# Another order of the groups, evictions and transfers in the fused stage of a Mamba and mixture-of-experts layer

## The reference

```
h = layernorm(x) * (1 + ca) + sa
x = x + ga * mamba(h)
h = layernorm(x) * (1 + cb) + sb
x = x + gb * moe(h)
```

```
delta = softplus(dt @ dt_proj_w.T + dt_proj_b)
h_t = exp(delta_t * A) * h_(t-1) + delta_t * u_t * B_t
y_t = sum over the 16 states of h_t * C_t
out = (y * silu(res)) @ out_proj_w.T
```

## Time and profile before

| | |
|---|---|
| median of 3 runs | 2546.36 us |
| the profiled execution | 2546.36 us, its span 2544.5 us |
| TensorE, VectorE, GpSimd, ScalarE busy | 2219.1, 1938.2, 1934.6, 1400.8 us |
| mean granted TensorE clock | 0.896 |
| DMA, mean | 88 GB/s |

### The profile page before, as it was taken

The page is one execution under the profiler, slowest core; times in us unless marked ns, Lnnn a source line. Parts: engine busy times, 40 slices in busy tenths (PEclk is TensorE's granted clock), DMA queues, the critical chain, the costliest instruction groups (busy, mean ns, idle before and its releaser), DMA issues. The chain is left out here.

```text
span 2544.5 us, 31166 instructions
## 1 busy us (share of the span) xinstructions
PE 2219.1 (87%) x7664; PEld 1058.8 (42%) x7665; DVE 1938.2 (76%) x2068; ACT 1400.8 (55%) x2474; POOL 1934.6 (76%) x830
## 2 busy tenths in 40 slices
PE   7769898999989898989898999989866639999997
PEld 3223343434434343444343434434333435565664
DVE  2799899998989898989899999989898162222222
ACT  3666666667575767667566667675745222222221
POOL 0699888899988898989788899989899014555553
PEclk9779889898989898989889898989787869999999
DMA  3534242424232333334242424232321062222221
GB/s 117 175 89 101 68 111 59 101 70 108 78 92 76 85 82 86 93 87 122 59 114 59 101 67 110 77 94 76 78 80 34 25 203 80 85 84 83 84 88 44
DMA packets 149400, 224.39 MB, mean 88 GB/s; under 512 B 48227, under 2 KB 85617, under 8 KB 145138
## 3 DMA queue, kind: packets, MB, share of 16 engines
q1 hardware_dynamic: 136914, 186.63, 27.8%
q0 software_dynamic: 12320, 35.93, 4.7%
HBM read 99.48 MB, written 31.47 MB: 51 GB/s over the span
## 5 line engine op out<-in xcount | busy, mean ns | idle before, releaser
L1004 POOL TENSOR_TENSOR hs<-hs,c_rep 128x2048 f32<-128x2048 f32 x256 | 1156.8, 4535 | 75.6 <-ACT state L738 75.4
L731 ACT ACTIVATE dA<-d_rep,a 128x512 f32<-128x512 f32 x1024 | 689.8, 686 | 478.0 <-DVE hs L839 474.7
L839 DVE TENSOR_TENSOR_SCAN hs<-dA,state,hs 128x512 f32<-128x512 f32 x768 | 928.8, 1265 | 23.0 <-ACT dA L731 18.8
L997 POOL TENSOR_TENSOR hs<-u_rep,b_rep 128x2048 f32<-128x2048 f32 x96 | 435.2, 4533 | 97.2 <-PE bank L507 89.4
L826 DVE TENSOR_TENSOR hs<-u_ps,b_rep 128x2048 f32<-128x2048 f32 x160 | 361.5, 2276 | 5.3 <-issue 5.1
L507 PE MATMUL bank<-hs,spread 128*32 128x512 f32 x2048 | 294.0, 726 | 36.9 <-POOL hs L1004 28.7
L839 DVE TENSOR_TENSOR_SCAN hs<-dA,hs 128x512 f32<-128x512 f32 x256 | 293.6, 1204 | 16.9 <-ACT dA L731 15.8
L478 PE MATMUL bank<-n,w1s 128*128 128x512 f32 x512 | 268.9, 662 | 27.8 <-DVE xpad L862 19.7
L1378 DVE TENSOR_TENSOR hid<-z,sg 128x512 f32<-128x512 f32 x70 | 48.4, 692 | 298.1 <-ACT sg L1356 298.1
L436 PE MATMUL bank<-xin,w_in 128*128 128x512 f32 x512 | 252.6, 629 | 13.6 <-ACT xin L583 7.4
L1296 PE MATMUL z<-w1r,hT 128*128 x560 | 260.5, 608 | 3.4 <-issue 2.3
...
(10 more groups left out here) (170 smaller groups left out, 2546.1 us busy)
## 6 DMA issues: line engine op xcount, KB each, us to landing
d_rep<-delta SPq DMA_DIRECT2D x1024, 64.0 KB, 2.0
u_rep<-us SPq DMA_DIRECT2D x384, 64.0 KB, 2.0
...
```

Source lines behind the costliest of these rows:

```text
L731: nc.scalar.activation(dA[:, u % ABANK, :], d_rep[:, q, :], ACT.Exp, scale=t["a"][:, u:u + 1]).then_inc(da_ready, 1)
L839: nc.vector.tensor_tensor_scan(hs[:, s % RING, g, :], dA[:, u % ABANK, :], hs[:, s % RING, g, :], state[:, u:u + 1] if m else 0.0, ALU.mul ...
L997: nc.gpsimd.tensor_tensor(hs[:, s % RING], u_rep[:, i % UBUF, :].unsqueeze(1).to_broadcast([P, NG, T]), b_rep[:, par, :].rearrange("p (g t ...
L1004: nc.gpsimd.tensor_tensor(hs[:, s % RING, :, :], hs[:, s % RING, :, :], c_rep[:, par, :].rearrange("p (g t) -> p g t", g=NG), ALU.mult).th ...
```

## The change

All five tables have other contents. The number of groups, their work and the code that works the tables are the same. What moves against the rest, by table:

- TensorE: XS 2, DB 3 and XS 3 go from sets 0 and 2 to set 1. OP 0 goes from set 5 to set 2, in front of CV 2, and OP 1 from set 5 to set 3. SUM 0 stands first in set 5. SUM 1 stands in front of GL, not behind it. DB 0 goes behind B 1, DB 1 between DT 2 and DT 3. T 1 goes behind a spread of u, into set 14 with all of A 1 to A 3 and Y 0.
- ScalarE: CV 2 is evicted in set 4 behind the first exponential, RS 0 and RS 1 in set 6 behind the first, XP in set 8 instead of 7, RB 1 in set 10 instead of 9; SRS stays at set 12. The norm N goes from set 12 to 13.
- VectorE: OP 0 and OP 1 each one set earlier, LN2 from behind OP 1 to behind the first scan of set 6, SUM 3, SUM 0 and SUM 2 a scan later or earlier, DB 0 and DB 1 earlier, LN a set later.
- GpSimd: the IN products behind other sets, IN 10 behind R2 in set 4, IN 2 of the next chunk in front of the weighing of set 14.
- DMA: U 5 leads the chunk, D 11 stands in front of BC, U 13 behind it, and the first ones of the next chunk in another order.

```diff
         plan = {
-            0: [(('Y', 1), -2), (('XS', 0), 1), (('XS', 1), 1), (('DB', 2), 0), (('XS', 2), 1), (('DB', 3), 0)],
+            0: [(('Y', 1), -2), (('XS', 0), 1), (('XS', 1), 1), (('DB', 2), 0)],
...
-            9: [(('GL', 0), -1), (('SUM', 1), 0), (('B', 0), -1), (('DB', 0), 1), (('B', 1), -1), (('B', 2), -1), (('B', 3), -1)],
+            9: [(('SUM', 1), 0), (('GL', 0), -1), (('B', 0), -1), (('B', 1), -1)],
...
         evict = {
-            4: [[], [], [(('CV', 1), 1), (('CV', 2), 1)], []],
+            4: [[(('CV', 2), 1)], [], [], []],
...
         vector = {
-            5: [[], [], [], [(('OP', 1), -1), (('LN2', 0), -1)]],
+            6: [[(('LN2', 0), -1)], [], [(('SUM', 0), 0)], []],
...
         gps = {
-            4: [(('R2', 0), -1)],
+            4: [(('R2', 0), -1), (('IN', 10), 0)],
...
-        transfers = [('ACC2', 0), ('W2', 0), ('XR', 0), ('D', 4), ('U', 5), ('D', 6), ('D', 5), ('U', 7), ('D', 8), ('D', 7), ('WO', 0), ('U', 10),
+        transfers = [('U', 5), ('ACC2', 0), ('XR', 0), ('D', 4), ('D', 5), ('W2', 0), ('D', 6), ('U', 7), ('D', 8), ('WO', 0), ('D', 7), ('U', 10),
```

More of the change, by code:

```diff
@@ L131, in fused_program @@
         plan = {
[4 rows of a table removed]
[4 rows of a table added]
             4: [],
[11 rows of a table removed]
[8 rows of a table added]
+            13: [(('SUM', 2), 0)],
+            14: [(('T', 1), 2), (('A', 1), -1), (('A', 2), -1), (('A', 3), -1), (('Y', 0), -1)],
+            15: []}
         evict = {
             0: [[], [], [], [(('XS', 0), 1), (('XS', 1), 1)]],
[15 rows of a table removed]
[L165 to L170, removed]
-            5: [[], [], [], [(('OP', 1), -1), (('LN2', 0), -1)]],
-            6: [[], [], [], [(('SUM', 0), 0)]],
+            1: [[], [(('XS', 2), 1)], [], [(('XS', 3), 1)]],
+            2: [[], [], [(('CV', 0), 1)], []],
+            3: [[], [(('CV', 1), 1)], [], []],
+            4: [[(('CV', 2), 1)], [], [], []],
+            5: [[], [(('CV', 3), 1), (('HALO', 0), 2)], [(('SU', 0), 1)], []],
+            6: [[(('RS', 0), 1), (('RS', 1), 1)], [], [], []],
+            7: [[(('N2', 0), -1)], [], [], []],
+            8: [[(('XP', 0), 1)], [(('RS', 2), 1), (('RS', 3), 1)], [(('T2', 0), -1), (('T2', 1), -1)], [(('DT', 0), 1), (('DT', 1), 1)]],
+            9: [[(('RB', 0), -1)], [], [(('E0', 0), 1)], []],
+            10: [[(('L0', 0), 1), (('RB', 1), -1)], [], [(('B', 0), -1), (('GL', 0), -1)], []],
+            11: [[], [], [(('B', 1), -1)], [(('B', 2), -1)]],
+            12: [[(('B', 3), -1), (('SRS', 0), 0)], [], [], [(('G', 0), -1), (('DT', 2), 1)]],
+            13: [[(('N', 0), 2)], [(('DT', 3), 1)], [], [(('GM0', 0), -1), (('E1', 0), 1)]],
+            14: [[], [], [], []],
+            15: [[(('L1', 0), 1)], [(('GM1', 0), -1), (('T', 0), 2)], [(('T', 1), 2)], []]}
+        vector = {
+            0: [[(('Y', 1), -2)], [], [(('DB', 2), 0)], []],
+            1: [[(('DB', 3), 0)], [], [], []],
+            2: [[], [], [(('SUM', 3), -1)], []],
+            3: [[], [], [], [(('OP', 0), -1)]],
+            4: [[], [], [], [(('OP', 1), -1)]],
+            5: [[], [], [], []],
+            6: [[(('LN2', 0), -1)], [], [(('SUM', 0), 0)], []],
             7: [[], [], [], []],
@@ L175, in fused_program @@
             9: [[], [], [], []],
[L176 to L180, removed]
+            10: [[(('SUM', 1), 0)], [], [], []],
+            11: [[(('LN', 0), 2)], [(('DB', 0), 1)], [], [(('DB', 1), 1)]],
+            12: [[], [], [], [(('A', 0), -1)]],
@@ L181, in fused_program @@
+            13: [[], [(('RC', 0), -1)], [], [(('SUM', 2), 0)]],
+            14: [[(('A', 1), -1)], [(('RC', 1), -1)], [(('A', 2), -1)], []],
             15: [[(('A', 3), -1)], [], [], [(('Y', 0), -1)]]}
         gps = {
[L183 to L186, removed]
-            4: [(('R2', 0), -1)],
-            5: [(('IN', 10), 0)],
+            0: [(('IN', 5), 0)],
+            1: [(('DU', 1), 0)],
+            2: [],
@@ L189, in fused_program @@
+            3: [(('IN', 7), 0)],
+            4: [(('R2', 0), -1), (('IN', 10), 0)],
+            5: [],
             6: [],
             7: [],
[L191 to L196, removed]
+            8: [],
+            9: [],
+            10: [(('G0', 0), -1), (('R', 0), 2), (('IN', 13), 0)],
+            11: [(('DU', 0), 1)],
+            12: [(('IN', 15), 0)],
@@ L197, in fused_program @@
+            13: [(('IN', 2), 1)],
             14: [],
-            15: [(('IN', 2), 1)]}
-        transfers = [('ACC2', 0), ('W2', 0), ('XR', 0), ('D', 4), ('U', 5), ('D', 6), ('D', 5), ('U', 7), ('D', 8), ('D', 7), ('WO', 0), ('U', 10),
-                     ('U', 13), ('D', 9), ('D', 10), ('BC', 0), ('X', 0), ('D', 12), ('D', 11), ('ROWS', 0), ('D', 13), ('LOG', 0), ('D', 15), ('U', 15),
-                     ('D', 14), ('U1', 2), ('D1', 0), ('D1', 3), ('D1', 2), ('D1', 1)]
+            15: []}
@@ L202, in fused_program @@
+        transfers = [('U', 5), ('ACC2', 0), ('XR', 0), ('D', 4), ('D', 5), ('W2', 0), ('D', 6), ('U', 7), ('D', 8), ('WO', 0), ('D', 7), ('U', 10),
+                     ('D', 9), ('D', 10), ('D', 11), ('BC', 0), ('U', 13), ('X', 0), ('D', 12), ('ROWS', 0), ('D', 13), ('LOG', 0), ('U', 15), ('D', 14),
+                     ('D', 15), ('D1', 2), ('D1', 0), ('U1', 2), ('D1', 1), ('D1', 3)]
         FIRST_TRANSFERS = [("D", 0), ("U", 2), ("D", 1), ("D", 2), ("D", 3)]
```

## The result

The changed kernel takes 2615.78 us, the median of 4 runs (2614.96 to 2616.44), against 2546.69 us of the kernel before: ratio 1.0271, 95% interval 1.0254 to 1.0289. It is 69 us slower, 4.3 us for each of the 16 chunks. Forecast were 2608 us, 61.5 us slower.

The account below looks back on a forecast made before the run. VectorE's work plus its waits for other engines was taken to set the chunk's length. Waits netted 5.0 us, the clock walk 4.1 a chunk; 15 x 4.1 = 61.5 us on 2546.4 gave 2608 us, range 2520 to 2638.

Parts of the forecast that it names:

- Step 1: TensorE before OP: parting both pairs of spreads of u adds two slots a chunk, 2 x 1.05 = 2.1 us.
- Step 2: VectorE, OP a set earlier: new waits of 1.1 us (OP 0), 0.9 (scan behind CV 2), 2.1 (OP 1), sum 4.1 us.
- Step 3: Layer norm 2 a scan later: GpSimd's reciprocal root starts 4.3 us later, delaying set 7's weighing, which SUM 1 needs.
- Step 4: TensorE, SUM 1 ahead of GL: starts only 0.9 us earlier, takes 5.85 us at the lower clock; VectorE's 4.5 us wait goes.
- The gaps stay: TensorE ahead of SUM 1: RS 3 still waits for XP's bank, from 959.0 until its eviction at some 961.6.
- Step 5: GL (3.55 us) between SUM 1 and B: B 0 starts at 983.4 against 980.8; new VectorE wait of 4.0 us.
- Step 6: ScalarE's two Silu and table loads before set 12's second exponential: scan 3.4 us late, VectorE waits 1.75 us against 1.10.
- Step 7: SUM 2 asked for a scan later, saving 0.85 us; A 1 1.6 us late behind one spread of u and T 1.
- Faster, by the clock: Rival, 0.17: OP 1 in time and no RS 3 stand let SUM 1 take 3.64 us; some 3 us less a chunk, 2501.
- Slower, but warm: Case, 0.22: SUM 1 takes 3.64 us at the upper clock, everything from B 2.2 us earlier; +1.9 a chunk, 2575 us.
- Only moved: Rival, 0.08: SUM 1's stall becomes OP's stalls (4.5 and 4.1 us), B no later; within 5 us of 2546.
- The signs: Residual waits 1 to 2 us, small SUM waits, dA waits some 80 us, GpSimd idle 2 to 4 us before layer norm 2.

Follow-up runs that it names:

- parted: Kernel before, with spread XS 3 worked in set 1 instead of 2 and RS 2 in set 6 instead of 7: 2546.45 us, ratio 1.0003.
- op_old: Changed kernel with the block of OP, CV, Silu of u and HALO at its old places on TensorE, ScalarE and VectorE: 2567.53 us, ratio 1.0075.
- ln2_early: Changed kernel with the statistics of layer norm 2 right behind the second residual addition again: 2584.18 us, ratio 1.0146.
- t_early: Kernel with old tables in sets 0 to 7, new in 8 to 15, changed to N in set 12 and T 1 right behind SUM 2: 2542.52 us.
- sum1_first: Kernel before with one edit, TensorE working SUM 1 in front of GL instead of behind it: 2512.91 us, ratio 0.9872.

## Why the prediction was right, point by point

The time was right in direction and size (2608 against 2616 us), and most steps stand in the trace. Some of them were of the wrong size, and the account of which of them is on the path was partly wrong. That the sum came so near is in part luck: the same walk gave the first half of the chunk 0 to 1 us alone and the second 1 to 2, where the runs show 3.5 and 0.

- *Step 1, the spreads.* Right as work (1.05 us each), wrong as a term: parted shows 0 us on the path.
- *Step 2, OP.* OP 0 was given 1.1 us and waits 0, OP 1 2.1 and waits 1.82, dA behind CV 2 0.9 and waits 1.04; 0.36 us at the spread behind OP 1 was not seen. In sum 3.2 against 4.1 us. op_old shows that this block is the root: 48 of the 69 us, of which an unknown part comes by way of RS 3 and the clock.
- *Step 3, layer norm 2.* GpSimd waits 2.55 us (the walk had its root 4.3 us late), and SUM 1 starts when set 7's weighing ends. ln2_early confirms it, 32 us.
- *Step 4.* SUM 1 at the lower clock (6.20 against 5.85), the stand for XP's bank 3.38 against 2.6, the wait at SUM 1 down from 4.5 to 0.64 us. Right. "The gaps stay" was not: the stand in front of RB (2.34 us) is gone, and the clock, back up behind RS 3 (1.00 from 994 to 997), falls again from 997 on.
- *Step 5, B late by GL.* This step failed. The term was mis-sized: GL was carried over at 3.55 us, its length at the lower clock, and takes 1.95 behind SUM 1. The wait at dA is 2.00 us, not 4.0. The swap alone is a gain of 32 us (sum1_first), where the walk, with a late SUM 1, had it start B 2.6 us later (983.4 against 980.8).
- *Step 6, Silu.* 1.56 us against 1.75. *Step 7:* A 1 1.44 against 1.6, and the wait at SUM 2 falls by 0.57 us (0.85 to 0.28) where 0.85 was given. Right. The stand of 6.68 us of TensorE for N was not in the text; SUM 2 takes 5.83 us behind it, 5.34 before, and by t_early it can't be said what it costs.
- *The sum* was 15 x 4.1 = 61.5 us. From the first statistics of layer norm 2 to the last, 15 chunks, the kernel before takes 1988.57 - 230.60 = 1758.0 us and the changed one 2052.67 - 241.87 = 1810.8: 52.8 us, 3.5 a chunk. The two rows of the kernel before:

```profile
230.60 0.38 DVE L800 BATCH_NORM_AGGREGATE mv<-stats 128x2 f32<-128x6 f32 x4
...
1988.57 0.38 DVE L800 BATCH_NORM_AGGREGATE mv<-stats 128x2 f32<-128x6 f32 x4 [0.26 <-DVE stats L794]
```

And those of the changed kernel:

```profile
241.87 0.38 DVE L800 BATCH_NORM_AGGREGATE mv<-stats 128x2 f32<-128x6 f32 x4
...
2052.67 0.38 DVE L800 BATCH_NORM_AGGREGATE mv<-stats 128x2 f32<-128x6 f32 x4 [0.26 <-DVE stats L794]
```

The other 16 us lie at the ends, 11.3 before the first statistics and 5.0 behind the last, where the forecast had nothing (the first of them hold 4 to 5 us by which the statistics stand later within a chunk, and one more chunk of the loop). So a term a little too large and ends that were left out made up the 69 us between them, which is luck as well.
- *The rivals.* "Faster, by the clock" did not come, but its mechanism is real. It asked for OP 1 in time and no stand at RS 3; op_old has both, and SUM 1 takes the 3.64 us that it named in 6 of 13 chunks. There the dA waits outweigh it (2568 us, not 2501). The 32 us of sum1_first are another effect, a GL at the upper level, with SUM 1 no shorter; the changed kernel has that already (1.95 us). "Slower, but warm" and "Only moved" fell with SUM 1 at 6.20 us and a loss of 69.
- *The signs.* The residual rows wait 24.8 us in 13 chunks, the row of sums is 17.0 us, GpSimd stands 2.6 us at the statistics: all as named. The dA waits came to 62.8 us, less than the 80 named. Of the signs of being wrong none came whole: from SUM 1 to B the clock is low under SUM 1 and at its upper level from GL on.
